# One of four value gathers of a region issued by GpSimd instead of SyncE, in a windowed attention kernel on one core

## The reference

```
qkv = einsum(gn(x), qkv_w) + qkv_b;  q, k, v = split(qkv)
idx = top_k(mean_region(q) @ mean_region(k), 4)            # (8, 49, 4)
key_g, val_g = take_along_axis(k, idx), take_along_axis(v, idx)   # 4 * 64 keys a region
out = softmax(q * 256**-0.5 @ key_g) @ val_g               # 8 heads of 32
out = out + depthwise_conv3x3(v) + lepe_b
return x + einsum(out, out_w) + out_b
```

## Time and profile before

| | before |
|---|---|
| median of three runs | 1945.03 us (1942.28 to 1945.11) |
| profiled execution | 1938.21 us, span 1936.4 us |
| PE, PEld busy | 1792.1 us (93%), 1174.8 us (61%) |
| DVE, ACT busy | 1630.8 us (84%), 1584.8 us (82%) |
| POOL busy | 703.0 us (36%) |
| DMA | 211.71 MB, mean 109 GB/s |
| q1 (queue of SP's DMAs) | 141392 packets, 129.82 MB |
| q0 (queue of POOL's DMAs) | 21504 packets, 77.08 MB |

### The profile page before, as it was taken

One profiled execution on the slowest core, in us unless ns is written; L12 is line 12 of the kernel. 1 busy time (PEld: TensorE's weight loads), 2 busy tenths in 40 slices (PEclk: granted clock), 3 DMA queues, 4 the chain that ended last, 5 costly groups with the idle time before them and its releaser, 6 DMA issues.

```text
span 1936.4 us, 75294 instructions
## 1 busy us (share of the span) xinstructions
PE 1792.1 (93%) x25672; PEld 1174.8 (61%) x25672; DVE 1630.8 (84%) x3819; ACT 1584.8 (82%) x5017; POOL 703.0 (36%) x2088
## 2 busy tenths in 40 slices
PE   4778999999999999999999999999999999977777
PEld 3435666666666666666666666666666666655544
DVE  4587999898998999988988899988998888877554
ACT  2447999888998999888988899888998888867774
POOL 1002334433333434433334333433334333433332
PEclk9999999999999999999999999999999999989998
DMA  3222444343443444434434343434343333333332
GB/s 113 57 66 72 114 116 135 106 120 112 134 118 111 119 123 120 123 108 119 125 110 121 111 126 111 126 105 126 115 122 95 110 100 111 99 106 86 101 100 83
DMA packets 163271, 211.71 MB, mean 109 GB/s; under 512 B 17760, under 2 KB 143824, under 8 KB 162896
## 3 DMA queue, kind: packets, MB, share of 16 engines
q1 hardware_dynamic: 141392, 129.82, 23.4%
q0 software_dynamic: 21504, 77.08, 13.7%
HBM read 155.45 MB, written 51.38 MB: 107 GB/s over the span
## 4 chain that ended last, share of the span: by engine, by line
SPq 46%; PE 30%; issue 9%; DVE 8%; DMA 5%; ACT 3%; POOLq 0%; DVEq 0%; ACTq 0%
SPq L232 34%; PE chunk_bank L750 10%; SPq L207 10%; PE pt_bank L827 6%; PE s_bank L816 4%; PE o_bank L841 4%; DVE lepe L515 3%; PE chunk_bank L763 3%; DMA v_sel<-v_dram 2%; DVE neg_max L610 2%; DMA v_dram<-v_stage 1%; PE chunk_bank L739 1%; SPq L222 1%; ACT probs L426 1%; PE chunk_bank L779 1%
## 5 line engine op out<-in xcount | busy, mean ns | idle before, releaser
L426 ACT ACTIVATE probs<-s_bank,neg_max 128x256 f32<-128x256 f32 x1568 | 734.4, 478 | 186.8 <-DVE neg_max L610 182.0
L282 POOL COPY k_sel<-k_all 128x128 f32 x1568 | 400.4, 299 | 1033.2 <-PE s_bank L816 1029.6
L515 DVE SCALAR_TENSOR_TENSOR lepe<-v_band,taps,lepe 128x448 f32<-128x448 f32 x896 | 618.0, 706 | 18.2 <-POOL v_band L298 5.8
L610 DVE TENSOR_REDUCE neg_max<-s_bank 128x2 f32<-128x512 f32 x784 | 506.3, 686 | 119.6 <-PE s_bank L816 112.1
L750 PE MATMUL chunk_bank<-xn,wqkv 128*128 128x448 f32 x1344 | 592.3, 549 | 14.9 <-ACT q_all L409 5.1
L433 ACT COPY probs_t<-pt_bank 128x512 f32<-128x512 f32 x784 | 469.4, 599 | 49.3 <-PE pt_bank L827 48.7
L827 PE MATMUL pt_bank<-ident,probs 128*128 128x128 f32 x3136 | 492.0, 280 | 13.3 <-ACT probs_t L433 12.4
L827 PEld LDWEIGHTS pt_bank<-ident,probs 128*128 128x128 f32 x3136 | 360.9, 141 | 154.7 <-issue 93.7
L426 ACT ACTIVATION_READ_ACCUMULATOR probs<-s_bank,neg_max 128x1 f32 x1568 | 322.5, 206 | 0.0
L841 PEld LDWEIGHTS o_bank<-probs_t,v_sel 128*32 128x32 f32 x12544 | 195.9, 111 | 185.3 <-issue 129.1
L750 PEld LDWEIGHTS chunk_bank<-xn,wqkv 128*128 128x128 f32 x1344 | 219.4, 192 | 119.4 <-issue 109.6
(11 more groups left out here) (57 smaller groups left out, 1384.4 us busy)
## 6 DMA issues: line engine op xcount, KB each, us to landing
v_sel<-v_dram SPq DMA_DIRECT2D x1568, 64.0 KB
x_in<-x_dram POOLq DMA_DIRECT2D x56, 448.0 KB, 4.9
v_dram<-v_stage SPq DMA_DIRECT2D x112, 224.0 KB
resid<-x_dram POOLq DMA_DIRECT2D x56, 448.0 KB, 4.5
out_dram<-resid POOLq DMA_DIRECT2D x56, 448.0 KB, 3.8
wqkv<-w_qkv_dram SPq DMA_DIRECT2D x1, 768.0 KB, 7.0
wout<-w_out_dram SPq DMA_DIRECT2D x1, 256.0 KB, 7.0
idx_row<-top_idx SPq DMA_DIRECT2D x8, 0.8 KB
```

The costliest lines, as they stand in the source:

```text
L282: last = pool.tensor_copy(k_sel[:, r % K_SLOTS, :, RT * j:RT * (j + 1)], k_all[:, b % 2, :, bass.ds(reg[j] * RT, RT)])
L426: act.activation(probs[:, u, :], s_bank[:, u, 0:KEYS], ACT.Exp, bias=neg_max[:, r % 2, u:u + 1], accum_out=denom[:, r % 2, u:u + 1]).then_ ...
L515: ins = dve.scalar_tensor_tensor(row, v_band[:, n % BANDS, k, t // 3:t // 3 + RS, t % 3:t % 3 + W], taps[:, k, t:t + 1], row, ALU.mult, AL ...
L610: dve.tensor_reduce(neg_max[:, r % 2, 2 * hf:2 * hf + 2], s_bank[:, 2 * hf:2 * hf + 2, 0:KEYS], AX.X, ALU.max, negate=True).then_inc(max_d ...
```

## The change

For all regions but the first two of an image, SP issues three gathers (j = 0 to 2). The fourth (j = 3) is issued by POOL, at the end of gather_keys, on a semaphore of its own, v_last_in, one for each slot of v_sel. Before it POOL waits for the stores of the image and for attn_done as SP does. attend(r) on PE waits for both semaphores; the new function gathers(r) gives how many of either a slot has had so far. For the first two regions of an image SP issues all four.

```diff
+BY_POOL = TOPK - 1
+def gathers(r):
+    same = range(r % V_SLOTS, r + 1, V_SLOTS)
+    first = sum(1 for q in same if q % NREG < 2)
+    return TOPK * first + BY_POOL * (len(same) - first), len(same) - first
...
+        v_last_in = [sem(f"v_last_in{i}") for i in range(V_SLOTS)]
...
-                for j in range(TOPK):
+                for j in range(TOPK if r % NREG < 2 else BY_POOL):
...
                 last.then_inc(k_sel_done, 1)
+                if r % NREG >= 2:
+                    pool.wait_ge(v_stored, 32 * NWIN * (b + 1))
+                    if r >= V_SLOTS:
+                        pool.wait_ge(attn_done, r - V_SLOTS + 1)
+                    half = RT * (BY_POOL % 2)
+                    pool.dma_start(v_sel[half:half + RT, r % V_SLOTS, BY_POOL // 2, :],
+                                   v_dram[b % 2][:, bass.ds(reg[BY_POOL] * RS, RS), :]
+                                   ).then_inc(v_last_in[r % V_SLOTS], 16)
...
-                pe.wait_ge(v_sel_in[r % V_SLOTS], 16 * TOPK * (r // V_SLOTS + 1))
+                by_sp, by_pool = gathers(r)
+                pe.wait_ge(v_sel_in[r % V_SLOTS], 16 * by_sp)
+                if by_pool:
+                    pe.wait_ge(v_last_in[r % V_SLOTS], 16 * by_pool)
```

## The result

The changed kernel takes 2214.9 us at the median (2212.9 to 2215.6) against 1944.4 us for the kernel before, timed beside it: a ratio of 1.140 (95% interval 1.138 to 1.141), 270.5 us slower. Forecast were 2095 us, 2045 to 2130. The direction and the mechanism were right, the size was not: 150 us of loss were foreseen, and 270 came.

The account below looks back on a forecast made before the run. PE's pace was taken as the bound, with SP needing about as long. From 1938.2 us, less 22.5, plus 168 and 6, came 2089.7; with most of the 6.8 us median offset, 2095 us was forecast, range 2045 to 2130.

Parts of the forecast that it names:

- SP's relief: In 376 regions SP drops one gather; PE's net waits for v_sel return: 22.5 us gained, bounds 10 and 33.
- The chain's 46% for SP: SP's issuing held 46% of the span in the chain that ended last; its worth was read from the waits instead.
- Order of the queues: In 42 rows POOL's halo waits for an attend, delaying DVE's tap 4.7 us and the next maximum 4.0: 168 us lost.
- Rivals 1 and 2: 1: wait hidden, only SP's relief left, 1922 us, chance 0.04; 2: part of the wait won back, 2050 us, chance 0.12.
- The wait without an issue: POOL's wait for the attend alone: the 4.0 us a row without the 0.17 and 0.71 us of issuing.
- The issue: POOL's fourth gather in 376 regions: 0.17 us register work plus 0.71 us issue, bounds 0.4 and 1.4.
- PE has nothing to pull ahead, so the whole 4.0 passes on: In the 42 rows PE is full and works in order, so each delay of 4.0 us reaches the next scores.
- POOL is idle 2.9 us a step, so one more microsecond does not make it the bound: POOL idles about 2.9 us before each group of key copies, so another microsecond a region does not make it the bound.
- 6 us for the last rows: Seven rows with s % 7 = 6: a store follows an attend and two more issues, 1 us each, bounds 0 and 12.
- Rivals 3 and 4: 3: POOL's issue 1.2 to 1.4 us, 2116 to 2124, chance 0.12; 4: several-microsecond lock at each issue, 2149, chance 0.03.

Follow-up runs that it names:

- e5: The kernel before with SP issuing three gathers a region (four in a few) and the fourth left out, POOL doing nothing instead: 1916.6 us.
- e11: The kernel before with only POOL's added wait for the attend (SP issues all gathers), plus 24 transposes on PE in the long step: 2048.2 us.
- e6: The changed kernel with 24 identity transposes added on PE in the stall of 42 rows of windows: 2163.6 us.

## Why the prediction was right or wrong

The chain of kernels e5, e11, e6, changed splits the loss: 1945 - 29 (e5) + 132 (e11) + 115 (e6) + 51 (changed) = 2214. From e5 to e11 comes the wait, with the clock held up; to e6 the issue moves to POOL; to the changed kernel the clock is let go. e11 still has SP's lateness in the last image, 207.7 us from its first attend to its last against 198.7 in e5, so that about 9 us move from the 132 to the 115.

- **SP's relief: right.** 22.5 forecast, 28.9 measured, within the bounds of 10 and 33. The chain's 46% for SP was indeed worth 1.5% of the time.
- **Order of the queues: right.** The halo in 42 rows waits for the attend, DVE for the halo, the scores for DVE; 221 us of idle time in 47 places against 190 in 42. Rivals 1 and 2 fell: nothing was hidden, nothing was won back.
- **The wait without an issue: nearly right.** From the forecast's own terms 4.0 - 0.17 - 0.71 = 3.1 us a row; measured 2.8 (7.00 to 7.06 against 4.23).
- **The issue: mis-sized, the first step that failed.** I added 0.17 + 0.71 = 0.88 us; the halo's start moved 1.22 us (0.10 to 1.32 after the attend). The 0.71 was within its bounds and even too high. The 0.5 us between register work and issue I had put at nothing, though POOL's loads of x in the kernel before show it (0.53 us). With the longer taps the long step grew by 1.5 us, so the stall is 4.3 and not 4.0: since the wait was priced too high and the issue too low, the two errors nearly cancel, and this step alone makes only 13 us of the miss.
- **"PE has nothing to pull ahead, so the whole 4.0 passes on": true, but not all.** I looked for what could be won back after a stall and not for what a stall sets off. This is the step that failed most: the clock took 51 us (e6), 1.5 us a row. The kernel before had shown it: in its last image, where PE is busy for less of the time, it is granted the lower clock in more stretches than elsewhere (seven of the nine). I had no term for it.
- **"POOL is idle 2.9 us a step, so one more microsecond does not make it the bound": true and beside the point.** POOL did not become the bound; its reads moved by a step's fraction onto DVE's taps, and I had put what POOL and DVE share outside the issue at nothing. Column 5 alone is 42 x 0.84 = 35 us (a third of which the shorter adds give back), and the last rows of the images lose another 1.7 us each (5.39, 5.56 and 5.14 against 4.95, 4.76 and 4.69). The forecast had 6 us for the last rows, for another reason (a later store).
- Rivals 3 and 4 named a longer issue and a lock at the issue. Neither happened in that form: the issue took 0.57 us, and 1.08 with the pause before it, still less than rival 3's 1.2.

About 15 us of the 124 that the issue costs in all (115 + 9) are in none of these lines. Part of them lies in the first rows of the images (six take 219.3 us in e6 and 207.1 in e11, of which column 5 is 5); why stays open. Against the forecast of 2095 the miss of 120 us is then 13 for the long step, 51 for the clock, 35 for column 5 and 6 more in the last rows, less 6 of relief; some 20 are not assigned.

## What to carry to other kernels

When a wait is added to an in-order queue, list everything behind it, find the user with the least slack, and place the wait behind that; here a halo with 0.03 us to spare made 214 of 270 us. Price a move to another engine not only by its idle time but by when its other work will then run, and what runs beside it on SBUF at that moment. And a stall on PE can cost more than its length, here 1.5 us on 4.3: look for the granted clock in the step after it. When an issuing queue is nearly the bound, first make its own work cheaper: fewer index loads gave more here than moving a gather away.

## What the runs showed of the hardware

- On SP, loading eight numbers from SBUF into registers takes 1.05 us where four take 0.82; on POOL four take 0.32.
- On POOL an issue that finds the engine idle starts 0.5 us after all waits and register work have ended: 0.51 for the gathers with an address from a register, 0.53 for the loads of x with fixed addresses. It then takes 0.57 us for 64 KB where the large plain loads take 0.71.
- 24 transposes that compute nothing, put into a stall of PE, made the kernel 51 us faster; the stall stayed at 8.55 us, and the stretches at half clock fell from 48 to 12.
- DVE's L655 with two inputs in SBUF took 1.1 us instead of 0.3 beside one of POOL's adds of 0.74. POOL's key copies took 505 ns instead of 294 beside such an instruction of DVE. L628 and L646, which read PSUM, were not touched.
